# DLRM tower on one core: batch chunks of 4, 4, 4, 2 and 2 tiles in place of four of 4, with the table lookups spread over all products

## The reference

```python
e = stack([tbl_f[ids[:, f]] for f in range(26)], axis=1)      # 2048 x 26 x 128
sd = einsum('bfd,bd->bf', e, dense)
ss = einsum('bfd,bgd->bfg', e, e)                             # pairs f < g are kept
h = concatenate([dense, sd, pairs(ss), dense], axis=1)        # 2048 x 607
h = maximum(h @ W_top1 + b_top1, 0.0)                         # 512 wide
h = maximum(h @ W_top2 + b_top2, 0.0)                         # 256 wide
y = h @ W_top3                                                # 2048 x 1
```

## Time and profile before

| | |
|---|---|
| median of three runs | 390.95 us (389.22 to 391.73) |
| the profiled execution's own time | 391.43 us |
| its span, first to last instruction | 389.6 us |
| mean granted TensorE clock | 0.965 |
| PE busy / POOL busy | 343.8 us (88%) / 265.4 us (68%) |
| DVE busy / ACT busy | 242.3 us (62%) / 191.2 us (49%) |

### The profile page before, as it was taken

How to read it: one execution, slowest core, us unless ns; L and a number is a source line. 1 busy time by engine, 2 the same in 40 slices (tenths; PEclk the granted TensorE clock), 3 DMA queues, 4 the chain that set the end, 5 groups by cost and what they waited for, 6 DMA issues and landing times.

```text
span 389.6 us, 12408 instructions
## 1 busy us (share of the span) xinstructions
PE 343.8 (88%) x5434; PEld 262.9 (67%) x5434; DVE 242.3 (62%) x475; ACT 191.2 (49%) x298; POOL 265.4 (68%) x279
## 2 busy tenths in 40 slices
PE   2899985999999997799999987899999988635996
PEld 0566664787788875688788864788788865434873
DVE  0799995587998642688998633488997541102420
ACT  3366665776133328685123258485133158842333
POOL 6777787777777777777777777777777777770000
PEclk9999997899999999999999999899999999958899
DMA  7996113243332214242432214233333212220000
GB/s 193 261 259 168 47 48 102 64 102 93 92 102 87 52 51 96 84 113 84 111 77 88 54 52 120 66 110 82 108 83 88 53 54 57 59 52 16 2 0 0
DMA packets 20090, 33.41 MB, mean 86 GB/s; under 512 B 7908, under 2 KB 10468, under 8 KB 20038
## 3 DMA queue, kind: packets, MB, share of 16 engines
q0 software_dynamic: 8704, 17.84, 18.3%
q1 hardware_dynamic: 11333, 14.78, 13.8%
HBM read 32.60 MB, written 0.01 MB: 84 GB/s over the span
## 4 chain that ended last, share of the span: by engine, by line
PE 71%; POOL 10%; issue 9%; DVE 4%; ACT 3%; DMA 2%; POOLq 0%; SPq 0%; ACTq 0%; DVEq 0%
PE late_bank L462 12%; PE late_bank L534 12%; PE late_bank L463 10%; POOL rows L441 10%; PE gram_bank L501 9%; PE turn_bank L482 6%; PE turn_bank L462 5%; PE turn_bank L463 5%; PE spare_bank L568 2%; PE gram_bank L568 2%; PE spare_bank L634 2%; DVE one_hot L807 2%; ACT turned L325 2%; PE turn_bank L515 2%; DMA rows<-in_tbl_dram,index 2%
## 5 line engine op out<-in xcount | busy, mean ns | idle before, releaser
L441 POOL DMA_INDIRECT rows<-in_tbl_dram,index x272 | 264.5, 973 | 85.1 <-issue 79.8
L809 DVE TENSOR_TENSOR one_hot<-table_ids,row_number 125x512 fp32r<-125x512 int32 x216 | 133.9, 682 | 23.2 <-PE turn_bank L463 15.6
L325 ACT COPY turned<-turn_bank 128x512 f32<-128x512 f32 (+1 forms) x72 | 70.2, 1030 | 36.5 <-PE turn_bank L482 33.2
L462 PE MATMUL late_bank<-one_hot,table_hi 125*128 125x512 f32 x192 | 81.2, 423 | 1.0 <-DVE table_lo L885 1.0
L463 PE MATMUL late_bank<-one_hot,table_lo 125*128 125x512 f32 x192 | 76.6, 399 | 0.0
L501 PE MATMUL gram_bank<-turned 128*27 128x26 f32 x4096 | 55.3, 195 | 15.1 <-issue 14.8
L501 PEld LDWEIGHTS gram_bank<-turned 128*27 128x27 f32 x4096 | 45.9, 109 | 31.6 <-issue 29.4
L482 PE MATMUL turn_bank<-ident,rows 128*128 128x128 f32 x288 | 47.1, 296 | 16.4 <-DMA rows<-in_tbl_dram,index 6.6
L482 PEld LDWEIGHTS turn_bank<-ident,rows 128*128 128x128 f32 x288 | 35.0, 150 | 27.2 <-issue 15.6
L296 DVE COPY gram<-gram_bank 124x208 f32<-124x208 f32 x32 | 12.0, 374 | 65.6 <-PE gram_bank L501 65.5
L462 PEld LDWEIGHTS late_bank<-one_hot,table_hi 125*128 125x128 f32 x192 | 36.6, 191 | 14.6 <-issue 3.8
(11 more groups left out here) (73 smaller groups left out, 338.8 us busy)
## 6 DMA issues: line engine op xcount, KB each, us to landing
table_ids<-in_ids_by_table_dram SPq DMA_DIRECT2D x27, 256.0 KB, 3.2
rows<-in_tbl_dram,index POOLq DMA_INDIRECT x272, 2.7
turned<-in_tbl_dram SPq DMA_DIRECT2D x6, 448.0 KB, 11.8
looked_up<-in_tbl_dram SPq DMA_DIRECT2D x3, 448.0 KB, 5.6
rows<-in_r_dense_features_dram SPq DMA_DIRECT2D x16, 64.0 KB, 3.2
gram<-in_W_top_dram SPq DMA_DIRECT2D x1, 702.0 KB
gram<-in_W_top_dram SPq DMA_DIRECT2D x1, 512.0 KB
turned<-in_tbl_dram SPq DMA_DIRECT2D x6, 52.0 KB
```

Source lines behind the costliest of these rows:

```text
L325: copy(to[:, f0:f1], of).then_inc(rows_copied[n % 2], 1)
L441: pool.indirect_dma_start(out=rows[:, row % RING_ROWS, :], out_offset=None, in_=tables[f], in_offset=bass.IndirectOffsetOnAxis(ap=index[:, ...
L462: pe.matmul(bank, table_hi[:, s, k, :], hot, start=k == 0, stop=False)
L809: last = nc.vector.tensor_tensor(hot, table_ids[0:RK, (c * LOOKUPS + s) % ID_SLOTS, :], row_number[0:RK, k:k + 1].broadcast_to([RK, CHUNK] ...
```

## The change

1. The chunks have 4, 4, 4, 2 and 2 tiles. All work of a two-tile chunk that took 512 columns takes 256. There are five chunks, so one set more of column turns, pair turns, layers and lookups (in all as many samples).
2. The lookups for the next chunk start at the second unit of the first tile. In a four-tile chunk there are 2, 3 and 3 blocks in the first tile, 4 a unit in the second and 3 a unit in the last two; in a two-tile chunk 6, 6, 6 in the first tile and 7, 7, 8, 8 in the second. The width of a block follows the chunk that it is for: those done in the third and the fourth chunk are 256 wide.
3. The first four turns of the next chunk's first tile follow the four units of layer 1, the fifth comes after layer 2's third step; nothing is turned between layer 2's last step and layer 3.
4. Lookups take other banks: the first six tables go round three banks, the last two use `gram_bank1` and wait for one another's copy.
5. Layer 3 has the samples as its stationary side and gives a column of 128 results for each tile. They gather in `y` (14 columns), are turned and stored once during the last chunk; the last chunk's own row is stored as before. The wait of the products for the store is gone.
6. Each id load is as wide as its chunk; their order on SP among the loads of dense rows is changed.

```diff
 TILES = 4
+SIZES = (4, 4, 4, 2, 2)
 ...
 BLOCKS = {
-    **{("unit", t, u): 4 for t in range(1, TILES) for u in range(UNITS)},
-    ("columns", 6): 4, ("pairs", 2): 4,
-    ("layer1", 0): 4, ("layer1", 1): 4, ("layer1", 2): 4, ("layer1", 3): 4,
+    2: {("unit", 0, 1): 6, ("unit", 0, 2): 6, ("unit", 0, 3): 6, ("unit", 1, 0): 7, ("unit", 1, 1): 7,
+        ("unit", 1, 2): 8, ("unit", 1, 3): 8, **LATE_BLOCKS},
+    4: {("unit", 0, 1): 2, ("unit", 0, 2): 3, ("unit", 0, 3): 3, **{("unit", 1, u): 4 for u in range(UNITS)},
+        **{("unit", t, u): 3 for t in (2, 3) for u in range(UNITS)}, **LATE_BLOCKS},
 }
 ...
-        def found_bank(s):
+        def found_bank(chunk, s):
 
-            return late_bank[s % 2][:] if s < LATE else whole_turn_bank[(s + 1) % 2]
+            if s > LATE and chunk.n > 0:
+                bank = gram_bank[1]
+            elif s >= LATE:
+                bank = whole_turn_bank[(s + 1) % 2]
+            elif chunk.n == 0:
+                bank = late_bank[s % 2]
+            else:
+                bank = (spare_bank, *late_bank)[s % 3]
+            return bank[:, 0:width(chunk)]
 ...
-            if n // 2 == y_unit // 2:
-
-                engine.wait_ge(stored, (c + 1) * DMA)
 ...
+            def layer3(chunk):
+
+                pe.wait_ge(h2_made, (chunk.n + 2) * N2)
+                for t in range(chunk.tiles):
+                    for k in range(N2):
+                        last = pe.matmul(y_bank[:, t:t + 1], h2[:, k, t * P:(t + 1) * P], w3_sb[:, k:k + 1],
+                                         start=k == 0, stop=k == N2 - 1)
+                last.then_inc(y_summed, 1)
 ...
                 for n in range(N1):
-                    layer1(c, n)
+                    layer1(chunk, n)
                     if more:
-                        look_up(c + 1, blocks_after("layer1", n))
+                        look_up(following, blocks_after(chunk, "layer1", n))
+                        turn_rows(following, 0, (n,))
                     for k in LAYER2_AFTER[n]:
-                        layer2(c, k)
+                        layer2(chunk, k)
                 if more:
-                    turn_rows(c + 1, 0, range(0, 2))
-                layer2(c, N1 - 1)
+                    turn_rows(following, 0, range(N1, TURNS))
+                layer2(chunk, N1 - 1)
                 if more:
-                    turn_rows(c + 1, 0, range(2, TURNS))
-                layer3(c)
+                    layer3(chunk)
+                else:
+                    last_layer3(chunk)
 ...
-            def work_off(c, more):
-                for t in range(TILES):
-                    awaited = not more and t == TILES - 2
+            def work_off(chunk, following):
+                more = following is not None
+                for t in range(chunk.tiles):
+                    awaited = not more and t == chunk.tiles - 2
                     for u in range(UNITS):
-                        if u == 0 and t == TILES - 2:
+                        if u == 0 and t == chunk.tiles - 2:
 
-                            place_found(act, c, TILES - 1)
+                            place_found(act, chunk, chunk.tiles - 1)
```

More of the change, by code:

```diff
@@ L96, with width, groups_in, steps_of @@
 SPREAD = 112
+Chunk = namedtuple("Chunk", "n first tiles")
+CHUNKS = [Chunk(n, sum(SIZES[:n]), tiles) for n, tiles in enumerate(SIZES)]
+def width(chunk):
+    return chunk.tiles * P
+def groups_in(chunk):
+    return chunk.tiles * GROUPS
+def steps_of(tiles):
+    return ([("unit", t, u) for t in range(tiles) for u in range(UNITS)] + [("columns", g) for g in range(COLS_TURNS)]
+            + [("pairs", k) for k in range(K_PAIRS)] + [("layer1", n) for n in range(4)])
 def offset(row):
@@ L431, in _ @@
                                pattern=[[-1, P]], channel_multiplier=1).then_inc(ident_made, 1)
-            for t in range(chunks * TILES):
+            for t in range(tiles):
                 if t in FIRST_TILES:
@@ new lines, in copy_output, with work_off @@
+            def copy_output(chunk, last):
+                act.wait_ge(y_summed, chunk.n + 1)
+                if last:
+                    nc.scalar.copy(last_y[:, 0:width(chunk)], last_y_bank[:, 0:width(chunk)]).then_inc(y_copied, 1)
+                else:
+                    nc.scalar.copy(y[:, chunk.first:chunk.first + chunk.tiles], y_bank[:, 0:chunk.tiles]).then_inc(y_copied, 1)
+            def work_off(chunk, following):
+                more = following is not None
+                for t in range(chunk.tiles):
+                    awaited = not more and t == chunk.tiles - 2
@@ new lines, in split_h1, with work_off @@
+            def split_h1(chunk, n):
+                wide = width(chunk)
+                dve.wait_ge(h1_hi_made, chunk.n * N1 + n + 1)
+                dve.wait_ge(h1_made, chunk.n * N1 + n + 1)
+                nc.vector.tensor_tensor(h1_lo[:, n % H1_SLOTS, 0:wide], h1_bank[n][:, 0:wide],
+                                        h1_hi[:, n % H1_SLOTS, 0:wide].bitcast(F32), ALU.subtract).then_inc(h1_split, 1)
+            def work_off(chunk, following):
+                more = following is not None
+                for t in range(chunk.tiles):
```

479 lines of the change are left out of this document (259 added, 220 removed).

## The result

The changed kernel takes 396.15 us (median of 5 executions, 394.63 to 399.75) against 391.73 us for the kernel before (5 executions, 389.22 to 393.97); ratio 1.0116, 95% interval 1.0071 to 1.0161. The interval lies above 1, so the loss is clear of the noise; by the forecast's own bounds (slower is over 394.9 us) it is slower, by a little, though the interval reaches under 1%. The forecast was 392.0 us and no change that can be told, range 383 to 401. One execution of all that follow, of hi_only, took 604.49 us where the nine others of that kernel took 388.91 to 391.58 us; it is left out. The profiled execution of the changed kernel is its slowest, 399.75 us with a span of 397.9 us; its other spans were 392.8 to 394.5 us.

What follows compares the result with a forecast made beforehand. It took POOL's gathers, then the last chunk's exposed tail, to bound the kernel before. From 267.4 us, 11.3 + 32.0 + 24.5 + 22.8 + 14.1 + 18.6 gave 390.7 us, 392.0 us on the median; range 383 to 401 us.

Steps and rivals of the forecast that it cites:

- The anchor: Start of the sum: the twelfth tile's last gathered row lands at 267.4 us, POOL's stream unchanged, five units left.
- The third chunk's products: Five units after the twelfth tile's rows: 8.8 us of work, 1.5 us for instruction refills, 1 us for low clock; 11.3 us.
- The third tail: Third chunk's columns and layers after its products: 37.97 us before, less narrower lookups and small layer changes; 32.0 us.
- The fourth chunk's products: PE and DVE closely coupled, 22.2 us, plus 1.6 us for ACT and 0.7 us for id loads; 24.5 us.
- The wait for ACT: Fourth chunk's products: PE's third turn needs the bank held up by ACT's 2.41 us copy; 1.6 us.
- The narrow matmul: Lookup matmul of 256 columns, taken at 0.12 us each, with a range up to 0.15 us.
- both slow rivals: After the twelfth tile, narrow matmuls cost 0.15 us: 400.1 us, chance 0.15; id loads of 4.3 us hold DVE: 398.8 us, 0.12.
- The fifth chunk's products: ACT paces the first tile, 9.4 us, then four units of 0.93 us and a 1 us refill; 14.1 us.
- The rival without waits: Priced stalls in the third to fifth chunks vanish: 382.5 us on the median, faster; chance 0.20.
- The rival that refills stop only pure products: No instruction refill waits where lookups are mixed into products: 389.5 us on the median; chance 0.10.
- The last chunk: Tail from last product to end shrinks from 29.3 to 18.6 us, giving 10.7 us back.
- What bounds the kernel before: POOL's gather stream, paced by nothing else, then the 512-sample tail sets the end; PE reaches the last chunk with spare time.

Runs made afterwards that it cites:

- hi_only: Changed kernel without the low-half table matmuls in lookups made for two-tile chunks; 390.01 us, ratio 0.9941 to the kernel before.
- after16: Changed kernel with one gather less in each tile, the row ahead used twice; 389.76 us, ratio 0.99 to the kernel before.
- warm: Changed kernel with 8 and 6 unread 256-column matmuls around layer 2's last step in the first three chunks; 398.13 us, ratio 1.015 to the kernel before.
- early: Changed kernel with the third chunk's lookup blocks moved to 8, 8, 2, 2 in its third tile and 1 a unit in its fourth; 394.82 us.
- phase: Changed kernel with 42 more 26-column matmuls ahead of the first chunk's products; 632.17 us on a chip where the kernel before took 678.12 us.
- before16: Kernel before with one gather less in each tile, the row ahead used twice; 390.27 us, ratio 0.993 to the kernel before.
- share: Changed kernel with two of ACT's five turned copies in the fifth chunk's first tile given to DVE; 398.76 us, ratio 1.0174 to the kernel before.
- act_later: Changed kernel with ACT's large copy in two-tile chunks put behind the first tile's second unit; 395.51 us, ratio 1.0087 to the kernel before.
- after_ring38: Changed kernel with 38 places in the ring of rows, not 44; 626.44 us on a chip where the kernel before took 678.12 us.
- before_ring38: Kernel before with 38 places in the ring of rows, not 44; 667.32 us on a chip where the unmodified one took 678.12 us.

## Why the prediction came out as it did

The time fell into the range, and the structure of the sum held; the median lies 4.2 us above the likeliest time, and where no change that can be told was forecast, a loss of 1.2% was measured. Step by step, in the profiled execution, whose span is 3.6 us longer than that of the median one (394.3 us):

| step | forecast us | measured us |
|---|---|---|
| twelfth tile's rows | 267.4 | 267.3 |
| third chunk, rest of the products | 11.3 | 12.8 |
| its tail | 32.0 | 32.7 |
| fourth chunk, products | 24.5 | 28.7 |
| its tail | 22.8 | 22.8 |
| fifth chunk, products | 14.1 | 14.7 |
| last tail | 18.6 | 18.8 |
| span | 390.7 | 397.9 |

- *The anchor*, the time at which the twelfth tile's rows let PE go on, was right to 0.1 us, but by luck: two errors cancel. The turn at 267.34 us, after an idle 3.52 us, is of the tile's fourth group, not its last, which stands two gathers earlier, so six units were left and not five. And POOL's stream didn't stay what it was: it is 1.6 us later than before from the twelfth tile to its end (the 204th gather begins at 266.24 us, not 264.66 us, the last at 351.75 us, not 350.13 us), mostly by one wait in the first chunk for PE to turn rows. after16 confirms that the gathers bind up to there and what comes after is added to them.

```profile
61.04 1.69 POOL L502 DMA_INDIRECT rows<-in_tbl_dram,index  x1 [3.40 <-PE turn_bank L547]
...
266.24 0.94 POOL L502 DMA_INDIRECT rows<-in_tbl_dram,index  x1 [0.30 <-issue]
```

- *The third chunk's products* are longer by that sixth unit (272.70 - 271.14 = 1.56 us in the timeline). The stop for instructions was 0.68 us, under the 1.5 us taken (the forecast's own figures, 2.7 refills of 4.1 us or more against 8.8 us of work, would have given over 2 us), and the low clock took that back.
- *The third tail*: layer 3's 16 short matmuls take 2.2 us (310.65 to 312.84 us) and the eight of the fourth tail 0.9 us; the sum had 0.5 us for those eight and no price of their own for the 16. The rest of the tail was right.
- *The fourth chunk's products* are the term that was mis-sized, by 4.2 us. The clock: half from 312 to 322 us. warm and after16 have the same work at full clock in 25.5 and 25.7 us, 1.0 and 1.2 us over the forecast, which leaves 3.0 to 3.2 us; 0.94 us of it is a stop for instructions, which warm doesn't have there (0.38 us in after16), and the rest, some 2.3 us, goes with the clock. The sum had a price for the clock in the third chunk only. The wait for ACT, 1.6 us in the sum, was 1.90 us in warm and after16 and 0.82 us here, where a slower PE comes later to its turn, so that wait hides a part of the clock's price; the id loads landed in 3.0 us and held nobody, where the sum had 0.7 us for them.
- *The narrow matmul* and the narrow one-hot cost what was taken, so both slow rivals are out: 0.116 us is far from 0.135, loads of 3.0 us (the median) are far from 4.3, and DVE waits for no id load in the chunks. The Trainium skill ("TensorE: Matmul & The Clock Gate", section "Back-to-back issue gap") has 262 cycles for 256 columns, at 2.4 GHz 109 ns; 0.116 us lies between that and the 0.12 us taken, and is nearer to the latter.
- *The fifth chunk's products*, 14.7 us against 14.1, are right by luck as well. What ACT paces took 8.0 us (364.39 to 372.37) and not 9.4, the stops for instructions 0.66 and 2.31 us and not 1.
- *The rival without waits* is out too: those stops came at more than their price. The rival that refills stop only pure products is mostly right for the fourth chunk (one stop of 0.94 us) and wrong for the third (0.68 us, and 2.44 us in early). The Trainium skill ("Runtime: NRT & Kernel Launch", section "Instruction fetch mechanics") calls the fetch mostly hidden; among long matmuls the traces agree (in the changed kernel none of 256 or 512 columns waits for its instructions), among matmuls of 26 columns they show stops of up to 2.5 us (2.31 us in the changed kernel, 2.51 us in phase).
- *The last chunk*: the tail gave back 10.5 us (29.3 to 18.8 us), as forecast (10.7 us). It had to be paid for with PE's spare time.
- *What bounds the kernel before* was told wrongly, though it cost the forecast nothing. The forecast had POOL's stream paced by nothing else in the program; but the ring ties it to PE (before16), and PE comes to the last chunk just when the ring is full. The forecast's "PE reaches the last chunk with time to spare" is right only in that it then waits for rows.

How much of the 4.4 us between the medians is the fourth chunk's clock can't be read, since only the slowest execution has a profile and share, whose profile has the same stretch (granted clock 0.53 from 310 to 321 us), is slower still. Why the clock is half for 10 us in these two, for some 7 us in hi_only, for 4 us or less in act_later and early and not at all in warm and after16 also stays open.

## What to carry to other kernels

A smaller last chunk shortens the exposed tail only by moving work onto the engine that had been waiting; first add up whether that engine's wait is larger than the extra chunk's cost. Before calling one engine's steady stream the bound, cut it and see: where a ring ties it to another engine, both can be the bound at once, and the sum of its waits (here 3.8 us) doesn't show it. In streams of very short matmuls, instructions are a resource: a few more of them far ahead can put a stop of 2 us into the part that is exposed, so compare variants by where their stops fall before believing a difference of that size.

## What the runs showed of the hardware that was not expected

- The stretches of low granted clock lie in other places from kernel to kernel, while the mean hardly moves: in warm's profile none from 308 to 322 us, but 0.57 over 16 us and 0.61 over 13 us elsewhere. The mean over the span was 0.961 in that profile and 0.966 in the changed kernel's, whose five executions have 0.961 to 0.974.
- On the chip where PE starts its short matmuls in small lots the order of the kernels turned round: after_ring38 has 0.9218 of the time of the kernel before. The two lines (waits of PE for its own instructions at the products, in before_ring38 and in after_ring38) differ by 57 us, more than the 35 us of span between them; the changed kernel puts lookups beside all products of its chunks, and its profile has 95 to 99 us from first products to columns in the second and third chunk, that of before_ring38 118 us. That the long matmuls give the instructions time to catch up is a guess from this and wasn't tested, nor is it known why the kernel before is 1.5% faster there with a smaller ring.

```profile
PE gram_bank L501 <- issue: 163.3, 227, 2.6
```

```profile
PE gram_bank L566 <- issue: 106.7, 179, 2.6
```
